# Routing of the first expert block inside the last state-space layer, weights loaded behind that layer

## The reference, cut to what matters

```python
# layer 0: a state-space block of four layers, then a mixture of experts
x = x + ga * _L0_attn_ref(h, ...)
h = _layernorm(x, axis=-1) * (1 + cb) + sb
x = x + gb * _L0_ffn_ref(h, P_w, U1, U2, U3, W1, W2, b2)
...
def _L0_ffn_ref(x, P_w, U1, U2, U3, W1, W2, b2):
    x_addr = x_flat @ P_w.T                        # 128 -> 64 addresses
    dw1 = _route_dense(x_addr @ U1.T, K, TAU)      # 12 experts, the best K=3, softmax over those
    dw2 = _route_dense(x_addr @ U2.T, K, TAU)
    dw3 = _route_dense(x_addr @ U3.T, K, TAU)
    h = _apply_mixture(x_flat, dw1, W1)            # sum over e of (x @ W1[e].T) * dw1[:, e], 128 -> 512
    h = gelu(h)
    y = _apply_mixture(h, dw2, W2)                 # 512 -> 128
    return y + dw3 @ b2
```

## Time and profile before

| what | value |
|---|---|
| median of 3 executions | 1206.99 (1205.53 to 1213.06) |
| the profiled execution | 1214.33, of which the span of its instructions 1212.5 |
| busy: PE, PEld | 1004.0 (83%), 674.4 (56%) |
| busy: DVE, ACT, POOL | 770.3 (64%), 527.8 (44%), 441.3 (36%) |
| granted TensorE clock, mean of the span | 0.886 |
| last `x_s4` of the state-space part | 344.43 |
| first expert matmul | 392.78 |
| first output matmul of the first block | 429.57 |

### The profile page before, as it was taken

The page is one execution under the profiler, slowest core; times in us unless marked ns, Lnnn a source line. Parts: engine busy times, 40 slices in busy tenths (PEclk is TensorE's granted clock), DMA queues, the critical chain, the costliest instruction groups (busy, mean ns, idle before and its releaser), DMA issues.

```text
span 1212.5 us, 20031 instructions
## 1 busy us (share of the span) xinstructions
PE 1004.0 (83%) x7982; PEld 674.4 (56%) x7982; DVE 770.3 (64%) x1348; ACT 527.8 (44%) x1215; POOL 441.3 (36%) x453
## 2 busy tenths in 40 slices
PE   6884998967273999999999578779799899969987
PEld 4643475745232878787877443335466534546643
DVE  7793475656567446463645778689656548946654
ACT  7616666373143312222120510047677536768642
POOL 7576216141037100000000424449654337945420
PEclk8866878888576999999999688989899999979899
DMA  4233806254152866428230400000112110012101
GB/s 106 53 68 65 145 6 127 59 92 89 36 210 49 142 97 104 104 67 128 45 72 0 168 0 1 0 1 1 36 36 54 49 70 27 1 36 55 41 14 35
DMA packets 59951, 75.45 MB, mean 62 GB/s; under 512 B 37448, under 2 KB 41940, under 8 KB 58140
## 3 DMA queue, kind: packets, MB, share of 16 engines
q1 hardware_dynamic: 59868, 74.31, 28.2%
HBM read 51.82 MB, written 1.51 MB: 44 GB/s over the span
## 4 chain that ended last, share of the span: by engine, by line
PE 57%; DVE 16%; POOL 12%; ACT 8%; issue 4%; DMA 2%; SPq 1%; POOLq 0%; DVEq 0%; ACTq 0%
PE psum L1334 7%; PE psum L1336 7%; PE psum L1335 7%; POOL rest L1586 3%; POOL rest L1576 3%; PE psum L1822 3%; POOL rest L1582 3%; PE psum L1829 2%; DVE main L1427 2%; PE psum L711 2%; PE psum L1838 2%; ACT rest L1520 2%; PE psum L1894 2%; PE psum L1875 2%; PE psum L785 2%
## 5 line engine op out<-in xcount | busy, mean ns | idle before, releaser
L427 POOL TENSOR_TENSOR kept<-kept 128x8 f32<-128x8 f32 x8 | 3.6, 446 | 342.9 <-DVE kept L388 342.9
L1520 ACT ACTIVATE rest<-psum,main 128x128 f32<-128x128 f32 x256 | 113.3, 481 | 11.5 <-POOL main L1597 11.5
L1170 ACT ACTIVATE x_high<-main 128x512 fp32r<-128x512 f32 x48 | 30.4, 633 | 174.5 <-DVE main L1251 174.5
L1612 POOL TENSOR_TENSOR rest<-rest,main 128x512 f32<-128x512 f32 x64 | 65.4, 1042 | 42.2 <-DVE main L1682 42.2
L1334 PE MATMUL psum<-x_high,w_low 128*128 128x512 f32 x192 | 75.8, 395 | 2.1 <-DVE x_low L1256 2.1
L1334 PE MATMUL psum<-hid_high,w_low 128*128 128x512 f32 x192 | 75.6, 394 | 0.7 <-DVE main L1275 0.7
L1335 PE MATMUL psum<-x_low,w_high 128*128 128x512 f32 x192 | 75.7, 394 | 0.0
L1336 PE MATMUL psum<-x_high,w_high 128*128 128x512 f32 x192 | 75.5, 393 | 0.0
L1335 PE MATMUL psum<-hid_low,w_high 128*128 128x512 f32 x192 | 74.8, 389 | 0.0
L1336 PE MATMUL psum<-hid_high,w_high 128*128 128x512 f32 x192 | 74.7, 389 | 0.0
L1676 DVE TENSOR_REDUCE main<-psum 128x4 f32<-128x512 f32 x64 | 41.4, 686 | 44.7 <-PE psum L1822 44.4
(11 more groups left out here) (343 smaller groups left out, 2794.2 us busy)
## 6 DMA issues: line engine op xcount, KB each, us to landing
rest<-share_d SPq DMA_DIRECT2D x4, 3072.0 KB, 21.7
main<-main SPq DMA_DIRECT2D x32, 256.0 KB, 6.4
main<-k_pad SPq DMA_DIRECT2D x16, 512.0 KB, 7.7
rest<-share_d SPq DMA_DIRECT2D x4, 2048.0 KB, 20.4
rest<-main SPq DMA_DIRECT2D x32, 256.0 KB, 3.6
main<-w_dram SPq DMA_DIRECT2D x2, 3072.0 KB, 14.0
main<-rest SPq DMA_DIRECT2D x32, 128.0 KB, 2.3
rest<-tables_dram SPq DMA_DIRECT2D x2, 2048.0 KB, 9.7
```

Of the source, the lines that this page charges most:

```text
L1520: last = A.activation(probs[:, p, 4 * r + m, :], bank[2 * p + r][:, m * P:(m + 1) * P], ACT.Exp, scale=row_scale[:, c, r, m:m + 1], bias=r ...
L1612: nc.gpsimd.tensor_tensor(probs[:, c % 2, four_heads], probs[:, c % 2, four_heads], row_sum[:, c % 2, four_heads].unsqueeze(2).to_broadcas ...
```

## The change

1. The norm is done block by block. The statistics of blocks 0 and 1 (`moe_dve_stats`) stand on DVE between the last layer's blocks, the transposes of block 0 on PE ahead of the last gate. ACT normalises and scales all four blocks, and copies the addresses and `weightT`, which was DVE's before.
2. The routing runs as three passes of `Routing`: block 0 alone, block 1 in pieces between experts 3 to 7 of the first expert block, and blocks 2 and 3 (`others`) on DVE after the last x part of the first block. ACT's first GELU waits for that pass (`moe_weight` 3), since the routing's tiles lie where the hidden parts go.
3. SP loads `pw`, `u`, `w1` and `w2` as soon as the last layer's large product on PE is over (`s4_tp_free`), and not after `x_s4`.
4. ACT's rounding of `w1` and `w2` is spread between the experts, DVE takes the first three remainders of `w1` (`w1_small`), POOL the other 21, and in the first block PE waits for them expert by expert.
5. The hardware loops of the experts are written out.

```diff
             else:
-                for b in range(BLOCKS):
-                    s4_dve_glu(dve, link, L, b)
+                link(V.memset(fresh, 1.0))
+                V.memset(fresh.rearrange("p c (r e) -> p (c r) e", r=ROUTERS)[:, :, 0:1], 0.0)
+
+                def added(b):
                     sl = slice(512 * b, 512 * b + 512)
                     dve.wait_ge(sem("s4_h"), L * BLOCKS + b + 1)
                     V.scalar_tensor_tensor(xT[:, sl], hT[:, sl], gate[:, 2:3], xT[:, sl], ALU.mult, ALU.add).then_inc(sem("x_s4"), 1)
+
+                s4_dve_glu(dve, link, L, 0)
+                added(0)
+                s4_dve_glu(dve, link, L, 1)
+                moe_dve_stats(dve, 0)
+                added(1)
+                s4_dve_glu(dve, link, L, 2)
+                moe_dve_stats(dve, 1)
+                added(2)
+                s4_dve_glu(dve, link, L, 3)
+                added(3)
...
@@ -852,6 +874,7 @@
                 for _ in range(4):
                     nc.tensor.matmul(bank[0][:, :], centre, hT[:, 0:512], start=True, stop=True)
             else:
+                moe_pe_tokens(pe, 0)
                 s4_pe_glu(pe, L, 3)
...
+            moe_act_norm(act, 0)
+            moe_act_out(act, 0)
+            moe_act_addr(act, 0)
+            moe_act_norm(act, 1)
+            moe_act_out(act, 1)
+            moe_act_addr(act, 1)
+            moe_act_exp(act, 0)
+            for e in range(ON_DVE):
+                w1_part(e)
+            moe_act_wT(act, 0)
+            for e in range(AHEAD):
+                share(e)
+                high(0, e)
+                w1_part(e + 3)
+            moe_act_norm(act, 2)
+            share(AHEAD)
+            for e in range(AHEAD, EXPERTS):
+                high(0, e)
+                if e + 3 < EXPERTS:
+                    w1_part(e + 3)
+                if e == 3:
+                    moe_act_norm(act, 3)
+                if e == 4:
+                    moe_act_exp(act, 1)
+                if e == 5:
+                    moe_act_out(act, 2)
+                if e == 6:
+                    moe_act_addr(act, 2)
+                    moe_act_out(act, 3)
+                if e == 7:
+                    moe_act_addr(act, 3)
+                if e >= 6:
+                    w2_part(e - 6)
+            moe_act_exp(act, 2)
+            moe_act_wT(act, 1)
+            act.wait_ge(sem("moe_weight"), 3)
+            hidden(0)
+            for e in range(EXPERTS - 6, EXPERTS):
+                w2_part(e)
+            moe_act_wT(act, 2)
+            moe_act_wT(act, 3)
+            for e in range(AHEAD):
+                high(1, e)
...
+        def moe_pool_scale(pool, b):
+
+            TT = nc.gpsimd.tensor_tensor
+            tiles = slice(4 * b, 4 * b + 4)
+            pool.wait_ge(sem("ln_aggr"), LN_B * TILES + 4 * b + 4)
+            TT(var_eps[:, tiles], mean_var[:, tiles, 1], eps_col[:, tiles], ALU.add).then_inc(sem("ln_eps"), 1)
+            TT(neg_means[:, tiles], mean_var[:, tiles, 0], neg_one[:, 0:4], ALU.mult)
+            pool.wait_ge(sem("ln_eps"), halves(LN_B) + b + 1)
+            TT(rstd[:, tiles], var_eps[:, tiles], neg_half[:, tiles], ALU.pow).then_inc(sem("ln_rstd"), 1)
+            pool.wait_ge(sem("ln_rstd"), halves(LN_B) + b + 1)
+            TT(shift_of[:, tiles], neg_means[:, tiles], rstd[:, tiles], ALU.mult).then_inc(sem("ln_shift"), 1)
...
+            class Routing:
+                def __init__(self, n):
+                    self.n, first, tiles = n, (0, 4, 8)[n], (4, 4, 8)[n]
+                    self.groups = tiles * ROUTERS
+                    self.wide = [P, self.groups, EXPERTS]
...
+                def best(self):
+                    dve.wait_ge(sem("moe_route_ps"), ROUTED[f"logit{self.n}"])
+                    link(V.tensor_copy(self.logit, bank[(4, 5, 7)[self.n]][:, 0:36 * self.tiles].rearrange("p (c e) -> p c e", e=36)))
+                    for k in range(self.groups):
+                        last = V.max(self.top8[:, k, :], g3(self.logit)[:, k, :])
+                    link(last)
...
+                def compared(self):
...
+            first, second, others = (Routing(n) for n in range(3))
+            first.best()
+            first.compared()
+            first.ranked()
+            first.chosen()
+            first.weighed()
+            w1_small(0)
+            moe_dve_stats(dve, 2)
+            dve.wait_ge(sem("ln_out_late"), halves(LN_B) + 1)
+            raw(0, 0)
+            w1_small(1)
+            raw(0, 1)
+            low(0, 0)
+            w1_small(2)
+            raw(0, 2)
+            low(0, 1)
+            moe_dve_stats(dve, 3)
...
                     low(b, e - 1)
+                    if b == 0:
+                        if e == 3:
+                            second.best()
+                        if e == 4:
+                            second.compared()
+                        if e == 5:
+                            second.ranked()
+                        if e == 6:
+                            second.chosen()
+                        if e == 7:
+                            second.weighed()
                 low(b, EXPERTS - 1)
                 dve.wait_ge(sem("moe_x_low"), (b + 1) * EXPERTS)
                 dve.sem_inc(sem("moe_share_free1"), 1)
+                if b == 0:
+                    others.best()
+                    others.compared()
+                    others.ranked()
+                    others.chosen()
+                    others.weighed()
...
+        def moe_pe_tokens(pe, b):
+
+            pe.wait_ge(sem("x_s4"), b + 1)
+            if b == 2:
+                pe.wait_ge(sem("s4_h"), S4_LAYERS * BLOCKS)
+            for t in range(4):
...
+        def moe_pe_back(pe, b):
+
+            pe.wait_ge(sem("ln_normed_late"), halves(LN_B) + b + 1)
+            if b == 0:
+                pe.wait_ge(sem("s4_h"), S4_LAYERS * BLOCKS - 1)
+            if b == 1:
+                pe.wait_ge(sem("s4_sig"), S4_LAYERS * BLOCKS)
+            for t in range(4):
...
+            if b == 0:
+                pe.wait_ge(sem("late_in"), 32)
+            if b == 2:
+                pe.wait_ge(sem("moe_share_copied"), SPREAD)
+            if b == 3:
...
+            moe_pe_tokens(pe, 1)
+            moe_pe_back(pe, 0)
+            moe_pe_tokens(pe, 2)
+            moe_pe_addr(pe, 0)
+            moe_pe_logits(pe, 4, (0,))
+            moe_pe_tokens(pe, 3)
+            moe_pe_back(pe, 1)
+            moe_pe_addr(pe, 1)
+            moe_pe_logits(pe, 5, (1,))
+            moe_pe_wT(pe, 0, 0)
+            pe.wait_ge(sem("moe_wT"), 1)
+            for e in range(AHEAD):
+                moe_pe_share(pe, e)
+            pe.wait_ge(sem("moe_share_copied"), 2)
...
                     pe.wait_ge(sem("moe_x_low"), b * EXPERTS + e + 1)
+                    if b == 0 and e >= ON_DVE:
+                        pe.wait_ge(sem("moe_w1_low"), e + 1 - ON_DVE)
...
+                    if b == 0:
+                        if e == 0:
+                            moe_pe_share(pe, AHEAD)
+                        if e == 2:
+                            moe_pe_back(pe, 2)
+                        if e == 3:
+                            moe_pe_addr(pe, 2)
+                            moe_pe_back(pe, 3)
+                        if e == 4:
+                            moe_pe_addr(pe, 3)
+                        if e == 5:
+                            moe_pe_logits(pe, 7, (2, 3))
+                        if e == 9:
+                            moe_pe_wT(pe, 1, 1)
...
+                if b == 0:
+                    pe.wait_ge(sem("moe_wT"), 2)
+                    pe.wait_ge(sem("moe_w2_low"), 2)
...
+                    if b == 0 and e == 3:
+                        moe_pe_wT(pe, 2, 2)
+                        moe_pe_wT(pe, 2, 3)
...
-            for dst, name in ((pw_sb, "pw"), (u_sb, "u"), (b2_sb, "b2")):
+            sp.wait_ge(sem("s4_tp_free"), S4_LAYERS)
+            for dst, name in ((pw_sb, "pw"), (u_sb, "u")):
                 sp.dma_start(dst, dram[name]).then_inc(sem("late_in"), 16)
             sp.dma_start(w1_low, dram["w1"]).then_inc(sem("moe_w1_in"), 16)
             sp.dma_start(w2_low, dram["w2"]).then_inc(sem("moe_w2_in"), 16)
-
-            sp.wait_ge(sem("moe_wT"), 1)
-            sp.dma_start(share_d[:, 0:512], weightT[:, 0:512]).then_inc(sem("to_dram"), 16)
-            sp.wait_ge(sem("to_dram"), 32)
+            sp.wait_ge(sem("late_in"), 32)
+            sp.wait_ge(sem("x_s4"), BLOCKS)
+            sp.dma_start(b2_sb, dram["b2"]).then_inc(sem("late_in"), 16)
+
...
-                    nc.gpsimd.tensor_tensor(w_low_s[:, e], w_low[:, e], w_high_s[:, e], ALU.subtract).then_inc(sem(f"moe_w{n}_low"), 1)
+            for b in range(3):
+                moe_pool_scale(pool, b)
+            for e in range(ON_DVE, EXPERTS):
+                pool.wait_ge(sem("moe_w1_high"), e + 1)
+                nc.gpsimd.tensor_tensor(w1_low_s[:, e], w1_low[:, e], w1_high_s[:, e], ALU.subtract).then_inc(sem("moe_w1_low"), 1)
```

(5 more changed lines are left out.)

309 lines of the change are left out of this document (163 added, 146 removed).

## The result

| | executions | median | ratio to the kernel before |
|---|---|---|---|
| kernel before, beside it | 12 | 1211.58 (1205.53 to 1215.29) | |
| changed kernel | 12 | 1204.87 (1202.03 to 1210.84) | 0.995 [0.9932, 0.9968] |
| changed kernel, second time | 10 | 1202.16, before 1212.16 | 0.9921 [0.989, 0.9952] |
| changed kernel, third time | 6 | 1204.11, before 1211.52 | 0.992 [0.9893, 0.9947] |

What follows compares the result with a forecast made beforehand. Ahead of the first expert a chain through one engine after the other bounds the kernel, then PE; 24.8 - 9.5 - 2.8 - 1.0 - 1.0 = 10.5 off the median 1206.99 gives 1196.5, range 1188 to 1205.

Steps and rivals of the forecast that it cites:

- Part 1: Last layer's end: +3.6 for block 3, not on the path; fourth `x_s4` from 344.4 to 348.0.
- Part 2: From the last layer's end to the first expert: first expert matmul at 368.0, 24.8 us earlier.
- only make room: Weight loads moved from 346 to 327 under the last layer's end: counted among the parts that come to nothing.
- Part 3: Expert loop of the first block: +9.5 (6.6 + 0.9 + 2.0), loop end at 412.8.
- the wait for ACT: First block's loop: address matmuls of blocks 2 and 3 need ACT's scaled blocks; 0.9 for the first, nothing sure for the second.
- DVE behind POOL: First block's loop: DVE and POOL get in each other's way; 2.0 taken, bounds 0 to 6.
- Part 4: GELU and outputs of the first block: -4.8, from the wait for `others` -2.8, clock -1.0, eight transposes -1.0.
- The loss of clock: Ahead of the first block's outputs PE idles some 3 us and may fall to half clock: -1.0, within 0 to -2.4.
- The parts that come to nothing: Weight loads only make room; written-out loops save hidden branch and register instructions; work moved to ACT is in part 2.
- Slower: PE stalls keep the expert loop's clock at half, each such expert costing 2.4; up to 16 slower, 1223; chance 0.06.
- All slack holds: First expert at 366, no loss to POOL, clock kept: gain 17.6, so 1189.5; chance 0.22.
- Given back: DVE and POOL alternate, six meetings count, GELU 5 later, outputs first at half clock: gain 2.9, 1204; chance 0.22.

Runs made afterwards that it cites:

- the combined kernel: Changed kernel with `others` spread over experts 7 to 10 and POOL's `w2` remainders behind the last x part; ratio to before 0.9899, repeated 0.9895.
- the filled kernel: Changed kernel with 13 unread 128x512 matmuls on PE between the first block's x parts and outputs; outputs 34.14, ratio to before 0.9882.

## Why the prediction was wrong, step by step

**The step that failed** is the base. The prediction says: "It lies 7.3 above the median of 1206.99, on which the forecast is made: 1196.5." The sum was made against the profiled execution and gives 1203.8 there. The three executions shown were a low draw: 78 have a median of 1211.5. On that base the same sum gives 1201.0, where 28 executions have 1204.0. So 4.5 of the 7.5 by which the forecast lay below this median was the base.

**The remaining 3.0.** The stretch explains 0.3 of it (10.2 against 10.5). The untouched parts hold 1.6 in the profiled executions: the last transpose started at 325.9 in the mean of four of before and 327.0 in three of after, and the rest behind the experts took 544.0 and 544.5. Those starts scatter from 322.7 to 328.1 in the kernel before alone, so a difference of 1.1 between means of so few is no finding. With the variants taken in, nine executions that begin as the changed kernel have the transpose at 327.5 in the mean and five that begin as the one before at 325.8, each group with a standard deviation of 2.3 to 2.5, and the rest behind is 544.1 and 544.2. So if anything is left it lies ahead of the transpose. The last 1.1 of the 3.0 is in no profiled execution, and most of the shortfall belongs to the first comparison, with its 5.5. Whether the change costs something ahead of its own code, or all of this is chance, stays open.

**Part 1.** The fourth `x_s4` was forecast at 348.0 and came at 347.4 on the same scale. DVE waited 0.79 for the transposes where I had 1.0, and the statistics of block 1 found no wait.

**Part 2.** The first expert was forecast 24.8 earlier, and the profile shows 24.7 (64.79 to 40.13). A match to 0.1 is luck in part: the weights of block 0 were ready 0.5 sooner than forecast (359.0 for 359.5), the way from there took 9.1 for 8.5, and other executions of the changed kernel had the first expert between 39.5 and 41.1. The order held as well: PE's address matmul of block 0 at 345.69, which is 347.8 (forecast 347.9), and the Exp behind ACT's work for block 1. That the loads "only make room" was wrong, since without them 3.3 to 4.2 of this is lost; it did not touch the sum.

The table load was weighed against the Trainium skill there: ScalarE: Activation LUTs, section "What ACT_TABLE_LOAD costs", puts a drain of about 1.38 us on top of the load. This time ACT was busy on both sides. Its copy ends at 353.91, the load starts at 353.93 and takes 1.28, and the Exp starts at 355.22. The trace shows no drain, so the price in the sum was right.

**Part 3.** The loop was forecast +9.5 and came out at +9.1 (35.29 to 44.40). The terms were off in both directions: insertions 7.3 for 6.6, the wait for ACT 0.7 for 0.9, and DVE behind POOL 0.5 as a wait of PE for 2.0. The run with the `w2` remainders put off gives 0.5 to 1.0 for the latter, though it removes the meetings with `w2`'s remainders only. Some 0.6 of the 9.1 has no row of its own. A single meeting costs about what I had taken, 1.1 at most (1.77 against 0.69) for 1.0, but most of them fell into slack. The Trainium skill names the condition (GPSIMD Engine Reference, section "Specifications": GpSimd shares its SBUF interfaces with VectorE and contends with DVE instructions that have two SBUF inputs). The trace agrees: operations with two SBUF inputs are slowed, while the reduction at 406.42 of the combined kernel, with one, is not.

**Part 4.** The gap was forecast at 4.3 and was 4.77, 3.3 more than before and not 2.8. The loss of clock was put at 1.0 inside 0 to 2.4 and was 2.1 to 2.8, as the filled kernel shows; this is the one term of the sum that was clearly too small. The eight transposes cost the 1.0 that they were given.

**The parts that come to nothing.** The written-out loops give 0.8, not nothing. The busy share of PE showed no loss because its window began with the first output matmul, and the loss lies just ahead of that, between a block's last x matmul and its first output.

**The sum against its terms.** In the first pair of profiles the stretch is 24.66 - 9.11 - 3.34 - 3.02 + 0.83 = 10.02: first expert, loop, gap, outputs, and later blocks. The forecast was 24.8 - 9.5 - 2.8 - 2.0 = 10.5. Gap and outputs cost 1.6 more than forecast, and the loop and the written-out loops gave 1.2 of that back. So the mechanism held, but the closeness of the two sums is in part luck.

**The rivals.** "Slower" needed the clock at half in the loop; it stood at 1.00 from 377 on. "All slack holds" wanted 17.6 in the stretch and failed at each of its terms: the first expert (24.7 earlier for 26.8), the loop (9.1 for 7.0), the gap and the clock. "Given back" named a total of 1204, which is what was measured, but by luck: it wanted 2.9 in the stretch, which held 10.2, and the total is that high mostly because the base was too low. In the version with `others` early DVE and POOL do give back what the gap gains.

## What to carry to other kernels

Cut the touched stretch out of the trace between two instructions that the edit leaves alone. Here it repeated within 2 us while totals of one kernel scattered by 15, and a forecast of a total is no better than its base: three executions were 4.5 off. When work is moved into a loop that PE bounds, count its insertions in full, count the stall at the loop's end twice (the wait itself and the slower clock after it), and look whether GpSimd is at work at that time. Moving DVE's work alone or GpSimd's alone gained 0.6 and 1.1 in the stretch, within its scatter, and moving both gained 4.5 in two executions.

## What the hardware did that I had not expected

- A 128x288 comparison on DVE took 1.55 beside GpSimd in place of 0.46, about the same 1.1 as a 128x512 one loses (1.77 against 0.69). In these rows a meeting costs by the instruction and not by the element, so a small operation loses the larger share. The 1.1 is the most that a meeting cost: a 128x288 multiply at 407.25 of the combined kernel, also beside GpSimd, took 0.61. Operations with one SBUF input (a reduction at 0.45) kept their time beside a busy GpSimd.
- PE idle for 3.39, behind 1.09 of small matmuls, came back at 0.50. After an idle time of 0.38 (combined) it came back at 1.00. The same scores of block 0 ran at 1.00 in two executions of the changed kernel and at 0.50 in the third, with the same waits ahead of them, and the way from the address matmul to the first expert was 22.0 there in place of 20.3.
- Identical instructions ahead of the change took from 322.7 to 328.1 us in four executions of the same kernel, a difference half the size of the effect under study.
